# Another order for the first image of an attention kernel, with two high parts of the first weights made on VectorE

## The reference

```python
h = group_norm(hidden_states, norm_gamma, norm_beta)
q = conv1x1(h, wq, bq)
k = conv1x1(h, wk, bk)
v = conv1x1(h, wv, bv)
...
attn = jnp.einsum('bci,bcj->bij', qf, kf) * scale
attn = jax.nn.softmax(attn, axis=2)
out = jnp.einsum('bcj,bij->bci', vf, attn).reshape(B, C, H, W)
out = conv1x1(out, wo, bo)
return residual + out
```

## Time and profile before

| | us |
|---|---|
| median of three runs (lowest, highest) | 1978.31 (1976.14, 1979.01) |
| the profiled execution, its own time | 1976.81 |
| its span, first to last instruction | 1974.8 |
| PE busy in the span | 1966.2 |
| DVE, ACT, POOL busy | 1630.7, 998.1, 327.0 |

### The profile page before, as it was taken

How to read it: one execution, slowest core, us unless ns; L and a number is a source line. 1 busy time by engine, 2 the same in 40 slices (tenths; PEclk the granted TensorE clock), 3 DMA queues, 4 the chain that set the end, 5 groups by cost and what they waited for, 6 DMA issues and landing times.

```text
span 1974.8 us, 29827 instructions
## 1 busy us (share of the span) xinstructions
PE 1966.2 (100%) x9924; PEld 1680.8 (85%) x9924; DVE 1630.7 (83%) x2285; ACT 998.1 (51%) x1528; POOL 327.0 (17%) x240
## 2 busy tenths in 40 slices
PE   9999999999999999999999999999999999999999
PEld 7888888888888888888888888888888888888887
DVE  8998896978969789696887969889698896978857
ACT  6474453645536464454644536446364553646443
POOL 2022120111202012020121201212011120212202
PEclk9999999999999999999999999999999999999999
DMA  7336252363414535054350533615236252363402
GB/s 250 128 150 171 76 148 96 149 170 127 114 77 155 164 149 139 31 173 146 149 159 32 173 125 149 170 66 151 102 149 170 108 124 87 150 169 149 92 31 43
DMA packets 55035, 254.66 MB, mean 129 GB/s; under 512 B 8160, under 2 KB 8160, under 8 KB 50400
## 3 DMA queue, kind: packets, MB, share of 16 engines
q1 hardware_dynamic: 36720, 221.01, 29.8%
q0 software_dynamic: 18288, 33.30, 10.8%
HBM read 213.39 MB, written 74.45 MB: 146 GB/s over the span
## 4 chain that ended last, share of the span: by engine, by line
PE 94%; DVE 0%; issue 0%; POOL 0%; ACT 0%; POOLq 0%
PE psum L419 32%; PE psum L420 31%; PE psum L421 31%; DVE red L1161 0%; DVE scores L1166 0%; POOL wide L394 0%; DVE scores L1152 0%; DVE scores L1351 0%; DVE scores L1220 0%; ACT room L730 0%; POOLq L393 0%; ACT scores L744 0%
## 5 line engine op out<-in xcount | busy, mean ns | idle before, releaser
L419 PE MATMUL psum<-big_hi 128*128 128x512 f32 x1056 | 412.0, 390 | 1.6 <-POOL big_lo L361 1.6
L420 PE MATMUL psum<-big_lo,big_hi 128*128 128x512 f32 x1056 | 411.6, 390 | 0.0
L421 PE MATMUL psum<-big_hi,big_lo 128*128 128x512 f32 x1056 | 411.4, 390 | 0.0
L419 PE MATMUL psum<-big_hi,h_hi 128*128 128x512 f32 x896 | 348.5, 389 | 0.0
L420 PE MATMUL psum<-big_lo,h_hi 128*128 128x512 f32 x896 | 348.5, 389 | 0.0
L421 PE MATMUL psum<-big_hi,h_lo 128*128 128x512 f32 x896 | 348.5, 389 | 0.0
L1152 DVE TENSOR_TENSOR scores<-psum,room 128x512 f32<-128x512 f32 x192 | 130.6, 689 | 199.6 <-ACT room L826 149.6
L826 ACT COPY room<-psum 128x512 f32<-128x512 f32 x192 | 113.1, 589 | 291.2 <-PE psum L421 291.2
L419 PE MATMUL psum<-w_split,h_hi 128*128 128x256 f32 x896 | 253.6, 283 | 0.3 <-ACT room L730 0.3
L420 PE MATMUL psum<-w_split,h_hi 128*128 128x256 f32 x896 | 253.6, 283 | 0.0
L421 PE MATMUL psum<-w_split,h_lo 128*128 128x256 f32 x896 | 253.6, 283 | 0.0
(11 more groups left out here) (134 smaller groups left out, 3445.3 us busy)
## 6 DMA issues: line engine op xcount, KB each, us to landing
w_split<-kept_t SPq DMA_DIRECT2D x15, 3584.0 KB, 11.8
w_split<-kept_v SPq DMA_DIRECT2D x15, 3584.0 KB, 11.3
room<-in_x SPq DMA_DIRECT2D x64, 512.0 KB, 3.5
out<-scores POOLq DMA_DIRECT2D x127, 256.0 KB, 6.8
room<-in_x SPq DMA_DIRECT2D x61, 256.0 KB, 5.7
red<-in_x SPq DMA_DIRECT2D x30, 256.0 KB, 3.7
wide<-in_x SPq DMA_DIRECT2D x30, 256.0 KB, 6.9
kept_t<-w_split SPq DMA_DIRECT2D x1, 3584.0 KB, 10.9
```

The costliest lines, as they stand in the source:

```text
L419: nc.tensor.matmul(o, a_hi, b_hi, start=start, stop=False, skip_group_check=True)
L420: nc.tensor.matmul(o, a_hi, b_lo, start=False, stop=False, skip_group_check=True)
L421: return nc.tensor.matmul(o, a_lo, b_hi, start=False, stop=stop, skip_group_check=True)
```

## The change

It gives the first image another order on every engine; the loop over the other images stays.

- PE: 8 fillers in place of 12; the bias products ahead of the transposes, into bank 7; the product of wv and wo starts on the first parts as they come; T starts on the first weights as they are split, in the order 4, 2, 5, 7, 6, 1, 3.
- ACT: issues the DMAs of gamma, beta and bo, which SP issued; wo's and wv's high parts are interleaved; the high parts of A22 and A12 come ahead of the weights'; five of the seven high parts of the first stage's weights.
- DVE: the other two (p = 5 and 7), right after the differences of the weights, by `tensor_copy`; the low part of wv's first quarter, which POOL made; the low parts of A22 and A12 ahead of the weights'; T's additions B22 and B21 behind the low parts of D4, B11, D2 and D1.
- The block S1 goes to `red` and no longer to `scores`, and the row half 1 of two intermediate results goes to another place in `room`.

```diff
+T_FIRST = (4, 2, 5, 7, 6, 1, 3)
+W_ACT, W_DVE = (2, 1, 3, 4, 6), (5, 7)
...
-H_FIRST = (A22, S1, A12, S3, S2, A11, S4)
+H_FIRST = (A22, A12, S1, S3, S2, A11, S4)
...
-        first_blocks = {**blocks, S4: red[:]}
+        first_blocks = {**blocks, S1: red[:], S4: red[:]}
...
-        snap_first = {"a": room[:, 1, :], "b": room[:, 3, :], "y": room[:, 5, :]}
+        snap_first = {"a": room[:, 5, :], "b": room[:, 3, :], "y": room[:, 1, :]}
...
-            for n, a in enumerate(vec_d):
-                sp.dma_start(vecs[:, n, :], a, allow_slow_non_contiguous=True).then_inc(vec_in, 16)
...
-            sp.wait_ge(wv_split, KC)
+            sp.wait_ge(wv_first, 1)
+            sp.wait_ge(wv_split, KC - 1)
             sp.dma_start(bv_rows, bv.partition_broadcast(P)).then_inc(bv_in, 16)
...
-            for o in range(KC):
+            for o in range(1, KC):
                 low_wv(o)
...
-            for _ in range(12):
+            for _ in range(8):
                 nc.tensor.matmul(bank[7], h_hi[:, 0, 0, 0:P], h_hi[:, 0, 0, :], start=True, stop=True,
...
+            pe.wait_ge(bias_step, 2)
+            for c in range(KC):
+                mm = nc.tensor.matmul(bank[2 * KC - 1][:, c:c + 1], wide[:, 0, cols(c)], primer[:, 0:1],
+                                      start=True, stop=True, skip_group_check=True)
+            mm.then_inc(bias_summed, 1)
...
             for n in range(KC):
+                if n == KC - 1:
+                    pe.wait_ge(t_bias_set, 1)
                 for c in range(KC):
                     mm = nc.tensor.transpose(bank[KC + n][:, cols(c)], wo_raw[:, c, cols(n)], ident[:])
                 mm.then_inc(wo_turned, 1)
...
                 if o == 0:
-                    pe.wait_ge(t_bias_set, 1)
-                pe.wait_ge(wot_split, KC if o == 0 else o + 1)
-                pe.wait_ge(wv_split, o + 1)
+                    pe.wait_ge(wv_first, 1)
+                else:
+                    pe.wait_ge(wv_split, o)
                 for c in range(KC):
+                    if o == 0:
+
+                        pe.wait_ge(wot_split, c + 1)
...
-                pe.wait_ge(wt_split, 7)
-                for p in T_ORDER:
+                pe.wait_ge(wt_split, 3)
+                for p in T_FIRST:
+                    pe.wait_ge(wt_split, W_AT[p])
                     pe.wait_ge(h_split, H_FIRST_AT[OF_H[p]])
...
+            for n in range(2):
+                act.dma_start(vecs[:, n, :], vec_d[n], allow_slow_non_contiguous=True).then_inc(scale_in, 16)
 
             act.wait_ge(bq_in, 16)
             for o in range(KC):
                 nc.scalar.activation(bias_terms[o], wk_raw[:, o, :], ACT.Identity,
                                      scale=bq_s[:, o:o + 1]).then_inc(terms_set, 1)
+            act.dma_start(vecs[:, 2, :], vec_d[2], allow_slow_non_contiguous=True).then_inc(vec_in, 16)
...
+            high_wot(0)
+            high_raw_wv(0)
+            for o in range(1, KC):
+                high_wot(o)
+            for o in range(1, KC):
+                high_raw_wv(o)
             for k in (2, 3):
                 normalise(0, k)
+            high_h(0, 0, True)
+            high_h(0, 1, True)
 
             act.wait_ge(wd_set, 4)
-            for p in W_ORDER:
+            for p in W_ACT:
                 high_wt(p)
-            high_h(0, 0, True)
...
             def first_parts():
 
+                for r in range(2):
+                    snap(0, r, 0, "a", T_FIRST_AT[4], True)
                 high_h(0, 2, True)
-                high_h(0, 1, True)
                 copy_wov(0)
                 copy_wov(1)
                 high_h(0, 3, True)
-                for r in range(2):
-                    snap(0, r, 0, "a", T_AT[4], True)
                 high_h(0, 5, True)
                 high_h(0, 4, True)
...
+                if o == 0:
+                    dve.wait_ge(wv_high, 1)
+                    nc.vector.tensor_tensor(wvs_lo[:, 0, :], wv_raw[:, 0, :], wvs_hi[:, 0, :].bitcast(F32),
+                                            ALU.subtract).then_inc(wv_first, 1)
...
+            for p in W_DVE:
+                nc.vector.tensor_copy(wt_hi[:, p - 1, :, :], wt_from[p]).then_inc(wt_copied, 1)
+            low_h(0, 0, True)
+            low_h(0, 1, True)
             for p in W_ORDER:
 
-                dve.wait_ge(wt_high, max(W_AT[p], 3))
+                dve.wait_ge(wt_high, max(W_ACT_AT.get(p, 0), 3))
+                if p in W_DVE:
+                    dve.wait_ge(wt_copied, W_DVE_AT[p])
...
-            low_h(0, 0, True)
...
             def make_first_t():
-                low_h(0, 1, True)
                 low_h(0, 2, True)
-
-                dve.wait_ge(bv_in, 16)
-                dve.wait_ge(vec_in, 16 * len(vec_d))
-                for c in (0, 1):
-                    row_dots(c)
                 low_h(0, 3, True)
                 sum_h(0, 2, True)
 
+                dve.wait_ge(bv_in, 16)
+                dve.wait_ge(vec_in, 16)
+                row_dots(0)
+                low_h(0, 4, True)
+                low_h(0, 5, True)
+                row_dots(1)
+
                 dve.wait_ge(wov_summed, KC)
                 add_t(0, 0, "D3", True)
-                low_h(0, 4, True)
-                low_h(0, 5, True)
                 sum_h(0, 3, True)
                 add_t(0, 1, "D3", True)
                 for c in (2, 3):
                     row_dots(c)
+                low_h(0, 6, True)
                 dve.wait_ge(bv_used, KC)
                 nc.vector.tensor_tensor(out_bias[:], wo_bv[:], bo_s, ALU.add).then_inc(biases_set, 1)
-                low_h(0, 6, True)
-                low_t(0, 0, "D3", True)
-                low_t(0, 1, "D3", True)
-                for name in C_ORDER[1:]:
-                    for r in range(2):
-                        add_t(0, r, name, True)
-                for name in L_ORDER[1:]:
-                    for r in range(2):
-                        low_t(0, r, name, True)
...
+                low_both("D3")
+                add_both("D1", "D2", "B11")
+                low_both("D4", "B11", "D2", "D1")
+                add_both("B22", "B21")
+                low_both("B22", "B21")
```

More of the change, by code:

```diff
@@ L32 @@
 T_AT = {p: n + 1 for n, p in enumerate(T_ORDER)}
+T_FIRST = (4, 2, 5, 7, 6, 1, 3)
+T_FIRST_AT = {p: n + 1 for n, p in enumerate(T_FIRST)}
 W_ORDER = (2, 1, 3, 4, 5, 7, 6)
 W_AT = {p: n + 1 for n, p in enumerate(W_ORDER)}
+W_ACT, W_DVE = (2, 1, 3, 4, 6), (5, 7)
+W_ACT_AT = {p: n + 1 for n, p in enumerate(W_ACT)}
+W_DVE_AT = {p: n + 1 for n, p in enumerate(W_DVE)}
 H_ORDER = (A22, A12, A11, S1, S3, S2, S4)
 H_AT = {x: n + 1 for n, x in enumerate(H_ORDER)}
-H_FIRST = (A22, S1, A12, S3, S2, A11, S4)
+H_FIRST = (A22, A12, S1, S3, S2, A11, S4)
 H_FIRST_AT = {x: n + 1 for n, x in enumerate(H_FIRST)}
@@ L230, in attention_program @@
             sem(n) for n in ("consts_set", "max_all", "sum_all", "rstd_set", "wv_split", "reduce_begun"))
-        primed = sem("primed")
+        wt_copied = sem("wt_copied")
+        primed, wv_first = sem("primed"), sem("wv_first")
         wkq_summed, wov_summed, wo_turned, bias_summed = (
@@ L647, in high_h @@
                 if a in (A11, A12, A22):
-                    act.wait_ge(h_full, 2 if first and a == A22 else count(b, KC, KC))
+                    act.wait_ge(h_full, 2 if first and a in (A22, A12) else count(b, KC, KC))
                 else:
@@ L719, in high_t @@
                 if name == "D4":
-                    act.wait_ge(t_summed, t_count(b, first, 7, r, T_AT[3]))
+                    act.wait_ge(t_summed, t_count(b, first, 7, r, (T_FIRST_AT if first else T_AT)[3]))
                     nc.scalar.copy(t_hi[:, OF_T[p], r, :], bank[alpha_t[r]][:]).then_inc(t_high, 1)
@@ L948, in sum_h @@
                     dve.wait_ge(h_full, count(b, KC, KC))
-                    nc.vector.tensor_tensor(blocks[S1], a21, blocks[A22], ALU.add).then_inc(h_summed, 1)
+                    nc.vector.tensor_tensor(blocks_[S1], a21, blocks[A22], ALU.add).then_inc(h_summed, 1)
                 elif n == 1:
@@ L953, in sum_h @@
                     dve.wait_ge(h_summed, count(b, 4, 1))
-                    nc.vector.tensor_tensor(blocks[S2], blocks[S1], blocks[A11], ALU.subtract).then_inc(h_summed, 1)
+                    nc.vector.tensor_tensor(blocks[S2], blocks_[S1], blocks[A11], ALU.subtract).then_inc(h_summed, 1)
                 else:
@@ L1029, in add_t @@
                 if name == "D3":
-                    dve.wait_ge(t_summed, t_count(b, first, 7, r, T_AT[5]))
+                    dve.wait_ge(t_summed, t_count(b, first, 7, r, (T_FIRST_AT if first else T_AT)[5]))
                     dve.wait_ge(t_snapped, t_count(b, first, 3, r, 1))
@@ L1034, in add_t @@
                 elif name == "D1":
-                    dve.wait_ge(t_summed, t_count(b, first, 7, r, T_AT[7]))
+                    dve.wait_ge(t_summed, t_count(b, first, 7, r, (T_FIRST_AT if first else T_AT)[7]))
                     dve.wait_ge(t_snapped, t_count(b, first, 3, r, 3))
```

(22 more changed lines are left out.)

25 lines of the change are left out of this document (9 added, 16 removed).

## The result

| | before | after |
|---|---|---|
| median, us (lowest, highest; runs) | 1978.26 (1975.64, 1979.01; 14) | 1982.34 (1980.81, 1983.36; 14) |
| ratio, 95% interval | | 1.0022 [1.0015, 1.0029] |
| the profiled execution, its span, us | 1976.81, 1974.8 | 1980.81, 1978.8 |

A forecast was written before the change was run, and what follows sets the result against it. PE was taken as the bound, with DVE as full in the first image. Later p = 1 arrival 2.2, DMAs 0.7 and clock 1.4 sum to +4.3 us on 1978.31: 1982.6, range 1978.8 to 1985.2.

The forecast's parts named there:

- likeliest case: First image: PE waits for DVE's late B21 addition and its clock falls, about +4.3 us; chance 0.45.
- The front: Start of first image: product of wv and wo at 21.8 us for 23.79, T at about 32.7 for 36.38.
- The copies: DVE's two new weight copies ahead of T: taken at 0.45 us each.
- The rival that they change nothing: DVE's copies: no effect, as T did not wait for ACT; counted inside the sum, no chance of its own.
- New waits on DVE: DVE during T: waits for ACT's high parts of S1, S3, S2, S4 total 2.2 us, for 0.45 before.
- The wait that turns the sign: First p = 1 score product: PE waits 3.7 us for DVE's B21 addition, going on 2.2 us later than before.
- The clock behind it: After PE's wait at p = 1: a clock fall costs 0 to 1.7 us, taken as +1.4.
- The DMAs on ACT, +0.7: Start: gamma, beta and output-bias DMAs beside the big loads delay wo by 0 to 0.9 us, taken +0.7.
- The shift lasts: Behind the p = 1 product: later work, to PE's product at 105.43 us, moves by the same amount.
- The clock holds: Rival at p = 1: the wait comes but the clock stays up, +2.9 us, 1981.2; chance 0.30.
- The check without any wait on DVE: First p = 1 product: with no DVE waits, B21's addition would end at 60.4 to 61.0 us.
- The floor: First p = 1 product: PE cannot pass before about 60.6 us, 0.3 ahead of before, if DVE starts at 20.34.

The follow-up runs named there:

- e7: Changed kernel with all seven high parts of the first stage's weights on ACT, no copies on DVE; 1981.60 us, 1.0024 of the kernel before.
- e1: Changed kernel with all of T's additions, B22 and B21 included, ahead of the low parts again; 1977.84 us, 1.0002 of the kernel before.
- e4: Kernel before with only the additions B22 and B21 moved behind the low parts of D4, B11, D2, D1; 1979.57 us, ratio 1.0014.
- e3: Changed kernel with 14 unused matmuls filling PE's wait for B21; 1980.69 us, 1.0018 of the kernel before.
- e6: Changed kernel with the DMAs of gamma, beta and the output's bias back on SP behind wo; 1981.22 us, 1.0024 of the kernel before.
- e2: Changed kernel with additions B22 and B21 between the low parts of D4, B11 and those of D2, D1; 1977.91 us, ratio to before 1.0005.
- e5: e2 with S1's and S3's high parts pulled ahead on ACT; 1977.23 us, 0.9999 of the kernel before.
- e9: e5 with ACT's three high parts of the second weights one behind each of the first three score snapshots; 1976.92 us, ratio to before 0.9999.
- e12: Changed kernel with the second image's first six loads issued after three, not seven, second-weight low parts; 1979.53 us, 1.0015 of the kernel before.
- e10: e9 with the second image's first six loads issued after three, not seven, second-weight low parts; 1974.98 us, 0.9992 of the kernel before.

## Why the prediction was right, and where its terms were off

The forecast of 1982.6 us stands 0.3 us from the measured 1982.34, and its likeliest case is what happened. Step by step:

- **The front.** Right. The product of wv and wo at 21.04 (forecast 21.8), the clock there at 1.00, T at 32.09 (32.7). `t_step` was held again, 0.74 us at 25.35, to the end of POOL's third low part (22.25 + 3.83 = 26.08), as forecast. DVE began its low parts at 19.70, 0.64 us ahead of before; "well ahead of 20.3" was to be a sign of being wrong outright, and this much did not undo the rest.
- **The copies.** 0.75 us for two, 0.37 each, for the 0.45 taken. The Trainium skill (VectorE: DVE Perf Modes, "Mode 2×_2P — use both read ports for one tensor") says that an fp32 copy within SBUF, having one input, can run at twice the rate of an instruction with two; the 0.37 us beside 0.61 go that way, at 1.6 times the rate. The rival that they change nothing is what e7 shows.
- **New waits on DVE.** Forecast 0.6, 0.8, 0.5 and 0.3 us for S1, S3, S2, S4; the trace has 0.52, 0.69, 0.52 and 0.30, and 0.60 ahead of the sum S1, which the prediction did not name. S at 53.44 (54.0).
- **The wait that turns the sign.** Right, and shown by taking the late additions out (e1) and by putting them alone into the kernel before (e4). 19 instructions from the end of S4's low part to the addition took 11.7 us (forecast 11.8); the wait is 3.28 us (3.7), the later arrival 1.44 (2.2 + 0.7).
- **The clock behind it.** Right in kind; mis-sized: 1.68 us for the 1.4 taken, just under the upper bound of 1.7. e3 removes it by filling the wait. It did not come through in full, though: e3's copies were 1.0 us earlier, as ACT was late as well, and a fall is worth about 1 us between the changed kernel's own executions.
- **The DMAs on ACT, +0.7.** Not borne out, and of the other sign in this pair of traces. The issues took 0.44, 0.54 and 0.42 us on ACT, the bias terms began at 10.68 and POOL's second sum ended at 15.83 + 1.28 = 17.11, ahead of the transposes, as taken; but the transposes began at 18.42, 0.64 us earlier than before, behind the bias products and with no wait for wo, and e6 gives no sign of a cost. By the Trainium skill's rule that I weighed there (DMA: Bandwidth & Descriptors, "Issuing engines are not separate DMA queues") the DMAs should have interleaved with the loads, and wo, by my working, should have landed later; no run here shows a landing delayed by it.
- **The shift lasts.** Right: POOL's reduction 3.38 us later, PE's product at 108.81 for 105.43. "Nothing behind gives any back" was too strong, though: the pieces' loads add a wait of 0.6 to 2.5 us of their own there, which varies by execution and lengthened the same stretch in e2, e5 and e9.

- **The rivals.** "The clock holds" is e3, 1980.69 us measured for 1981.2 worked out, and by the mean clock it came about in two of the changed kernel's 14 executions (1980.90 and 1981.31). The check without any wait on DVE put PE at 60.4 to 61.0 for p = 1; with the additions out of the way PE came at 60.71 (e1) and 60.08 (e2), and neither beat the kernel before. The floor counts all eight low parts ahead of the addition; e2 has four of them behind it, 2.4 us less, and so came below, while DVE's start was 0.45 us earlier there (19.89 for 20.34).

So 2.2 + 0.7 + 1.4 = 4.3 is in truth 1.44 + 1.68 + 0.26 in the first image and 0.7 in the pace of the others. Errors cancelled: the arrival at p = 1 was 1.5 us less late than 2.2 + 0.7, of which 1.3 is the DMA term (0.64 earlier for 0.7 later); the clock, the stretch to the reduction and the pace made up 0.3 + 0.26 + 0.7. That the sum came out within 0.3 us is luck in the sizes; the step that turns the sign is not.

## What to carry to other kernels

When an order on a full engine is changed, look for the one instruction that another engine waits for last, and count what now stands ahead of it. Of 4.3 us won at the front 2.3 were gone by S, where DVE had waited for ACT and PE for DVE, and eight instructions of 0.6 us ahead of an addition turned the rest into 1.4 us lost. A lead won upstream shows in the time only as far as every later hand-over can take it; here it ran out first on DVE, then on ACT, then on loads that were issued later than their room allowed, and each came to light only when the one ahead of it was gone. An idle wait of PE is dearer than its length when the clock falls in it, 1.68 us on top of 3.28 here.

## What the runs showed that was not expected

- After the wait of 3.27 to 3.31 us, PE's clock was at its lower level in each of the four traces that have it. By it PE lost 1.6 to 1.7 us in three (changed kernel, e7, e12) and 2.9 in e6, where the clock is at 0.50 from 63 to 69 us. Five of the 45 executions of these kernels are at 1.000, so it need not fall. After waits of 0.87 to 1.80 us at the same place it stayed at 1.00 (e1, e2, e4, e5, e9, e10). The early fall of the kernel before is not in e4, which has the same front and the same 1.65 us wait, so it differs between executions; 57 of 91 of the kernel before are below 1.000.
- A small strided DMA took 0.42 to 0.58 us to issue on ACT in the nine traces that have it there. On SP, behind the big loads, the first took 0.43 to 0.55 us and each further one 2.2 to 2.9, in four traces (the earlier trace rows and e6 among them).
- Loads of the same pieces, issued at the same step, made DVE wait 0.6 us in one trace and 2.5 in another, and 0 when issued 5 to 8 us earlier.
